# Holding the load queue for the first weight slice and interleaving transposes with weight pieces

## The reference

```python
# x: (2, 2048, 512); cond_8: (2, 8); all float32
masked_w = weight * mask[None]                       # (8, 512, 512)
w_bot = einsum('bg,got->bot', cond_8, masked_w)      # one 512x512 matrix per batch
h = einsum('bnt,bot->bno', x, w_bot) + bias          # conditioning
# bitlinear(x, w) = act_quant(x) @ weight_quant(w).T
#   weight_quant: scale = 1 / mean(|w|); w -> round to -1, 0, 1, divided by scale
#   act_quant: per row, 127 / max(|x|), round to int8 range, divided by scale
gate = silu(bitlinear(h, w_gate))                    # 512 -> 2048
up = bitlinear(h, w_up)                              # 512 -> 2048
out = x + bitlinear(gate * up, w_down)               # 2048 -> 512
```

## Time and profile before

| | |
|---|---|
| median of three executions | 454.75 us |
| the profiled execution | 453.42 us |
| its span | 451.6 us |
| TensorE busy | 434.9 us, 96% |
| VectorE busy | 366.4 us, 81% |
| ScalarE busy | 327.1 us, 72% |
| GpSimd busy | 154.4 us, 34% |
| HBM read, written | 40.11 MB, 8.39 MB |
| DMA, mean over the span | 155 GB/s |

### The profile page before, as it was taken

How to read it: one execution, slowest core, us unless ns; L and a number is a source line. 1 busy time by engine, 2 the same in 40 slices (tenths; PEclk the granted TensorE clock), 3 DMA queues, 4 the chain that set the end, 5 groups by cost and what they waited for, 6 DMA issues and landing times.

```text
span 451.6 us, 7215 instructions
## 1 busy us (share of the span) xinstructions
PE 434.9 (96%) x2186; PEld 232.7 (52%) x2186; DVE 366.4 (81%) x625; ACT 327.1 (72%) x448; POOL 154.4 (34%) x160
## 2 busy tenths in 40 slices
PE   4899998999999999999999999999999999999995
PEld 0234443444444455555655555655556565555654
DVE  0316579898956798799998999999999989999991
ACT  1216847785356776888888888888888888888861
POOL 0000170606099554232424324233341434414122
PEclk9999999999999999999999999999999999999999
DMA  7999997995420434352634526345353553535455
GB/s 281 402 401 415 412 252 160 339 279 121 102 48 10 78 77 109 103 116 77 159 69 134 119 75 150 67 133 118 91 134 75 141 107 103 116 93 142 86 148 139
DMA packets 104458, 69.78 MB, mean 155 GB/s; under 512 B 87281, under 2 KB 87537, under 8 KB 102897
## 3 DMA queue, kind: packets, MB, share of 16 engines
q1 hardware_dynamic: 103856, 67.39, 54.3%
q10 hardware_dynamic: 576, 2.10, 1.3%
HBM read 40.11 MB, written 8.39 MB: 107 GB/s over the span
## 4 chain that ended last, share of the span: by engine, by line
PE 44%; DMA 23%; DVE 12%; issue 11%; ACT 8%; SPq 1%; DVEq 0%; ACTq 0%
PE ps L888 12%; DMA wc<-wc 12%; PE ps L843 10%; PE ps L951 8%; PE ps L923 7%; DMA wc<-w_gate 4%; PE ps L881 4%; ACT wc L473 4%; DVE wc L733 3%; DVE wc L699 3%; DMA qT<-q_sb 3%; DMA wc<-wcond 2%; DMA wc<-w_down 2%; DVE p_part L751 2%; PE ps L856 1%
## 5 line engine op out<-in xcount | busy, mean ns | idle before, releaser
L888 PE MATMUL ps<-tern_up,qT 128*128 128x512 f16 x512 | 131.2, 379 | 0.6 <-DVE wc L733 0.6
L843 PE MATMUL ps<-w_bot,xT_sb 128*128 128x512 f32 x256 | 113.2, 595 | 2.3 <-DVE w_bot L636 1.6
L843 PEld LDWEIGHTS ps<-w_bot,xT_sb 128*128 128x128 f32 x256 | 48.0, 190 | 61.2 <-issue 57.5
L751 DVE TENSOR_REDUCE p_part<-wc 128x1 f32<-128x1536 f32 x64 | 77.9, 1218 | 1.7
L888 PEld LDWEIGHTS ps<-tern_up,qT 128*128 (+1 forms) x512 | 50.0, 98 | 55.3 <-DVE wc L733 1.3
L733 DVE TENSOR_TENSOR wc<-ps,xT_sb 128x512 f32<-128x512 f32 x104 | 71.3, 685 | 7.5 <-issue 3.6
L473 ACT ACTIVATE wc<-wc 128x1024 f16<-128x1024 f32 x64 | 67.0, 1051 | 4.6 <-DVE wc L796 2.8
L463 ACT ACTIVATE wc<-wc,p_scale 128x2048 f32<-128x2048 f32 x31 | 62.1, 2002 | 4.5 <-DVE p_scale L789 4.5
L951 PE MATMUL ps<-wc 128*128 128x256 f16 x480 | 62.2, 273 | 0.2 <-DVE wc L699 0.2
L699 DVE TENSOR_TENSOR wc<-wc 128x1024 f16<-128x1024 f16 x60 | 56.7, 945 | 3.8 <-DMA wc<-wc 2.7
L458 ACT ACTIVATE xT_sb<-ps,gate_unit 128x512 f32<-128x512 f32 x78 | 49.2, 684 | 11.7 <-PE ps L923 11.2
(11 more groups left out here) (93 smaller groups left out, 544.1 us busy)
## 6 DMA issues: line engine op xcount, KB each, us to landing
xT_sb<-xT SPq DMA_DIRECT2D x32, 256.0 KB, 7.5
x_res<-x SPq DMA_DIRECT2D x30, 256.0 KB, 2.9
out<-result SPq DMA_DIRECT2D x30, 256.0 KB, 2.4
wc<-wcond SPq DMA_DIRECT2D x12, 512.0 KB, 13.6
wc<-w_gate SPq DMA_DIRECT2D x4, 1024.0 KB, 17.7
wc<-w_up SPq DMA_DIRECT2D x4, 1024.0 KB, 13.4
wc<-w_down SPq DMA_DIRECT2D x4, 1024.0 KB, 7.3
wc<-wcond ACTq DMA_DIRECT2D x4, 512.0 KB, 7.7
```

Of the source, the lines that this page charges most:

```text
L751: nc.vector.tensor_reduce(p_part[:, par, i:i + 1], prod[:, par, 512 * lo:512 * hi], AX.X, ALU.max, apply_absolute_value=True).then_inc(par ...
L843: ins = nc.tensor.matmul(ps[:, t % COND_BANKS], xT_sb[:, t % XSLOTS, k], w_bot[:, t // HALF, k], start=(k == 0), stop=(k == KH - 1))
L888: ins = nc.tensor.matmul(ps[:, UP + i % 2], tile_of(s, k), tern_up[:, i, k], start=(k == 0), stop=(k == KH - 1))
```

## The change

SyncE waits for pieces 0 and 1 of slice 0 before it issues anything but y. The order of SyncE's loads after the bias is written out anew: w_gate 0 and 1 (after the mixing of slice 1), x 8 to 10, w_gate 2 and 3, x 11, and after the mixing of all slices w_up 0, transpose 0, w_up 1, transpose 1, the second mask, x 12, transpose 2, w_up 2, x 13, transpose 3, w_up 3, x 14; from tile 4 on x t + 11 and transpose t. ScalarE takes the sums of w_gate's pieces 2 and 3 after its rounds 0 and 1. TensorE's first sum stands before tile 9 instead of 8, in the bank of tile 11.

```diff
--- before.py
+++ after.py
@@ -25,11 +25,11 @@
 XSLOTS = 8
 COND_BANKS = 8
 LATE = TILES - 2
-AHEAD = 12
+AHEAD = 11
 HSLOTS = 3
 QSLOTS = 4
-SUM_TILE = (8, 14, 21)
-SUM_BANK = (10 % 8, 16 % 8, 23 % 8)
+SUM_TILE = (9, 14, 21)
+SUM_BANK = (11 % 8, 16 % 8, 23 % 8)
 ROUND = 12582912.0
 QMAX = 127.0
 FLOOR = 1e-5
@@ -217,6 +217,7 @@
                 sp.dma_start_transpose(qT[:, t], q_sb[:, t % QSLOTS]).then_inc(s_qT[t % QSLOTS], 16)
 
             sp.dma_start(y_sb[:, :], y_col).then_inc(s_small, 16)
+            sp.wait_ge(s_wc[0][1], 16)
             load_wc(0)
             for t in range(FIRST):
                 load_xT(t)
@@ -228,23 +229,29 @@
             for t in range(EARLY, XSLOTS):
                 load_xT(t)
             sp.dma_start(bias_sb[:, :], bias.partition_broadcast(P)).then_inc(s_bias, 16)
-            for a in range(PIECES):
-                if a % 2 == 0:
-                    sp.wait_ge(mix_psum, 2 * (a // 2 + 1))
-                load_raw(0, w_gate, a)
-            for a in range(PIECES):
-                if a % 2 == 0:
-                    sp.wait_ge(mix_psum, 2 * (a // 2 + 3))
-                if a == 0:
-                    for t in range(XSLOTS, XSLOTS + 3):
-                        load_xT(t)
-                if a == 2:
-                    for k in range(KH):
-                        load_mask(1, k)
-                    for t in range(XSLOTS + 3, AHEAD):
-                        load_xT(t)
-                load_raw(1, w_up, a)
-            for t in range(LATE):
+            sp.wait_ge(mix_psum, 4)
+            load_raw(0, w_gate, 0)
+            load_raw(0, w_gate, 1)
+            for t in range(XSLOTS, XSLOTS + 3):
+                load_xT(t)
+            load_raw(0, w_gate, 2)
+            load_raw(0, w_gate, 3)
+            load_xT(XSLOTS + 3)
+            sp.wait_ge(mix_psum, 2 * KH)
+            load_raw(1, w_up, 0)
+            transpose_q(0)
+            load_raw(1, w_up, 1)
+            transpose_q(1)
+            for k in range(KH):
+                load_mask(1, k)
+            load_xT(XSLOTS + 4)
+            transpose_q(2)
+            load_raw(1, w_up, 2)
+            load_xT(XSLOTS + 5)
+            transpose_q(3)
+            load_raw(1, w_up, 3)
+            load_xT(XSLOTS + 6)
+            for t in range(QSLOTS, LATE):
                 if t + AHEAD < TILES:
                     load_xT(t + AHEAD)
                 transpose_q(t)
@@ -588,9 +595,9 @@
                 for b in range(BATCH):
                     nc.scalar.activation(w_bot[:, b, k], ps[:, MIX], ACT.Copy, scale=half_on[:, b:b + 1]
                                          ).then_inc(half_copied, 1)
-            for a in range(PIECES):
-                abs_sum_piece(0, a)
-            abs_after = {3: (1, 0), 4: (1, 1), 5: (1, 2), 6: (1, 3), 12: (2, 0), 13: (2, 1), 14: (2, 2), 15: (2, 3)}
+            abs_sum_piece(0, 0)
+            abs_sum_piece(0, 1)
+            abs_after = {0: (0, 2), 1: (0, 3), 3: (1, 0), 4: (1, 1), 5: (1, 2), 6: (1, 3), 12: (2, 0), 13: (2, 1), 14: (2, 2), 15: (2, 3)}
             for t in range(LATE):
                 cond_round(t)
                 if t in abs_after:
```

## The result

The change makes the kernel slower: 456.89 us, median of 20 runs, against 453.53 us for the kernel before in 20 runs of its own; ratio 1.0071, 95% interval 1.0058 to 1.0084. I had forecast 453.6, that is 1.2 us less on the scale of the first three runs (454.75); measured are 3.4 us more. The range, 451.4 to 456.8 on the scale of 454.75, is 3.4 us less to 2.1 us more, so the result lies beyond it on the slow side.

The account below looks back on a forecast made before the run. TensorE, busy 434.9 of 451.6 us, was taken as the bound. A front shift of -0.3 and -0.9 at tile 16 made -1.2 us: 452.2 against the profiled 453.42, 453.6 on the runs' scale (454.75); range 451.4 to 456.8.

Parts of the forecast that it names:

- What bounds the kernel: Whole kernel: TensorE busy 434.9 of 451.6 us; loads or reorders win only its holes, and slice 2's supply is level with it.
- the hole that the prediction named: Front of the kernel: TensorE starts its products some 4 us earlier at best, then waits before slice 1's mixing.
- The hold: SyncE's wait for slice 0's first two pieces: gives slice 0 the engines, with no gap or at most 0.8 us.
- s: Shift of the whole front, set by the supply: taken as -0.3 us, between -2.1 and +0.8.
- two pieces (2.5 us) cover that: After SyncE wakes: slice 0's remaining two pieces cover the 2.0 us until SyncE's first data come.
- The gate pieces: w_gate's loads: piece 2 lands at 45.6 behind three x tiles; with ScalarE's order the mean comes 0.8 us earlier.
- Tile 8 issued at 38.71 can land at 41.3, so the queue doesn't run dry: SyncE's queue before w_gate's piece 2: gate pieces already queued, the second landing at 41.15, cover the wait for tile 8.
- rival B: SyncE's wait for tile 8: gate pieces 0 and 1 drain first, piece 2 comes too late; middle +1.6 us, 456.3; chance 0.15.
- deciding point (46.4): Landing time of w_gate's piece 2 at which the mean of w_gate comes no earlier than before.
- the gap: Start of the kernel: possible supply gap of 0.8 us when SyncE's first loads come after the hold.
- The transposes and w_up: Transposes between w_up's pieces: ScalarE's 7.09 us and TensorE's 1.23 us waits go; w_up's sum has 2 us to spare.
- Tile 16 next in line: TensorE at tile 16 waits 1.0 us instead of 0.64 for w_up's mean; of the 1.23 us only 0.9 remains.

Follow-up runs that it names:

- e12: Kernel of e3 with SyncE held until the first piece of slice 0 has landed instead of the second; 452.22 against 452.99 us, ratio 0.9969.
- e1: Kernel before with only SyncE's wait for two pieces of slice 0 added; 453.96 against 453.17 us, ratio 1.0004.
- e4: Changed kernel without the hold and with w_gate's pieces 2 and 3 ahead of x tiles 8 to 10; 451.58 against 453.17 us, ratio 0.9955.
- e3: Changed kernel, hold kept, with w_gate's pieces 2 and 3 issued ahead of x tiles 8 to 10; 452.51 against 453.17 us, ratio 0.9983.
- e2: Changed kernel without SyncE's wait for slice 0; 455.11 against 453.17 us, ratio 1.0039.
- e5: Second profile of the changed kernel, nothing altered; this execution took 458.71 us at a mean clock of 0.993.
- e10: Kernel of e8 with TensorE's tile 16 also waiting for VectorE to begin tile 14; 456.59 us.
- e8: Kernel of e4 with TensorE's first sum before tile 8 instead of 9; 450.84 against 453.16 us, ratio 0.9953.
- e9: Kernel of e8 with TensorE's tile 16 also waiting for VectorE to begin tile 13; 453.13 us.
- e6: Kernel before with only x tiles 8 to 10 issued between w_gate's pieces 1 and 2; 456.78 against 453.16 us, ratio 1.0078.

## Why the prediction was wrong

**What bounds the kernel: right.** TensorE's early start was worth nothing, because it then waits for the supply. The 3.0 us were gone by the end of slice 1's mixing, the hole that the prediction named, and slice 2, where the supply and TensorE are level, took the 0.9 us on top.

**The hold: wrong in sign, by a small amount.** I took s = -0.3 within -2.1 to +0.8; between the two first profiles it is +0.95. Over all profiles the products behind slice 3's mixing start at 35.86 to 36.51 in the five with a hold and at 34.88 to 35.58 in the nine without. The step that failed is "two pieces (2.5 us) cover that": SyncE's mask, issued at 6.5, landed 5.0 us later, the engines moved 249 GB/s from 8 to 12 us, and slice 2's last piece was 0.9 us late. That the first causes the last isn't shown (e12). By itself the hold costs nothing that can be measured (e1). Together with the transposes between w_up's pieces it costs 0.8 us at tile 16 and 0.9 in the medians (e4 against e3); in the order of the change it is 0.3% by the two ratios, and the profiles there don't separate it from scatter (e2).

**The gate pieces: this is the step that failed**, as the prediction put it: "Tile 8 issued at 38.71 can land at 41.3, so the queue doesn't run dry." I compared a landing (piece 1 at 41.15) with a landing. But piece 1 landed at 41.2 in both kernels, with the engines full before and with a mean share of 0.56 and then 0.29 after: a landing doesn't tell when the engines' work ends. (The trace has the mean of the 16 engines only, so what holds the last landing back isn't shown.) Tile 8's own 2.6 us were about right: issued at 39.59, it landed in 2.8. Piece 2 needed 6.7 us from its issue for 2.5 us of data, and landed 2.8 us after my 45.6: 0.9 because SyncE came to tile 8 later, 1.9 beyond my sum. That is rival B, whose place and deciding point (46.4) were named and which I gave 0.15. Its price was about right for the idle time (tile 16 later by 1.8; I had up to 2.1, to 2.9 with the gap).

**What no case held** is the clock. I priced an idle time of TensorE by its own length. In the 15 of 20 runs with a lower mean clock it cost more than that: 3.1 us more in e5 (20.47 for 17.41), 1.7 in e10. With 1.7 to 3.1 us added, B's sum would have been 3.5 us and more, beyond the end of my range (2.1 us more).

**The transposes and w_up: right.** ScalarE's 7.09 us for a slot and TensorE's 1.23 us are gone, w_up's sum was ready before TensorE came (71.38 without a wait), though by 1.0 us and not by 2: ScalarE's last sum ended at 70.4, where I had 68.5. **Tile 16 next in line: right.** Of the 1.23 us nothing could be kept without an earlier mean; with the gate pieces together, tile 16 starts at 78.61 in e4 and, without a stop, near 77.7 in e8, and the gains I had forecast for the whole (1.2 us) are there (1.6 and 2.3).

## What to carry to other kernels

A queue is dry when its engines are idle, not when its last load lands: before a wait is put in front of a load, look at the DMA share of the last microseconds ahead of the landing, and keep enough loads queued in front of the wait to last through it. On an engine whose clock follows its activity, price a wait by what the matrix work behind it then takes: those of 3.2 and 3.4 us here cost another 3.1 and 1.7 us beyond their length (e5, e10). Whether it is cheaper to split such a wait in two, no run tests. And a chain that has just lost its stop has a next member with its own date; here it was two means, and only moving both loads and sums together gave a gain.

## What the runs showed that I had not expected

The clock's fall doesn't hang on the length of the idle time alone: in the profiles 1.70, 2.21 (e2) and 2.93 us left it full, 3.16, 3.34 and 3.44 lowered it, and so did the 2.79 us of e1 (0.64 granted from 100 to 104 us). In the three runs of e9 with the lower clock no profile shows where it fell, so that stays open. Also open is why the DMA moves so little in two places: 249 GB/s from 8 to 12 us with the engines occupied (0.96), and 180 to 330 GB/s from 41 to 46 us, with loads queued again and a share of 0.72 to 0.91. The first stands in every profile with the long hold (249 to 273), the second, more or less, in each one with x tiles 8 to 10 ahead of w_gate's pieces 2 and 3 (e2, e5, e6), but no run takes either apart.
